# The state scan of a Mamba layer: all scan inputs made by TensorE from turned dt*u instead of half of them by VectorE

## The chip, the cores and the metric

One core of a Trainium2 chip runs one launch of a two-layer network. The metric is device time in microseconds (us) of that launch, the median of three runs. In the profile PE is TensorE (PEld its weight loads), DVE VectorE, ACT ScalarE, POOL GpSimd, SP the engine that issues the DMAs.

## The reference

The network is: normalisation, attention, normalisation, a mixture of experts; normalisation, a Mamba layer, normalisation, a second mixture of experts, on an input of 4 sequences x 1024 positions x 128 channels. The change touches the Mamba layer alone. Of it, this matters (256 inner channels, 16 states, rank 8):

```python
u = silu(causal_conv(xc))                          # (B, L, 256)
dt_low, Bm, Cm = split(u @ x_proj_w.T, [8, 24])    # 8, 16 and 16 columns
dt = softplus(dt_low @ dt_proj_w.T + dt_proj_b)    # (B, L, 256)
A = -exp(A_log)                                    # (256, 16)
for t in range(L):
    h = exp(dt[t][..., None] * A) * h + (dt[t] * u[t])[..., None] * Bm[t][:, None, :]
    y[t] = einsum('bdn,bn->bd', h, Cm[t])
y = (y + u * D) * silu(z)
```

## The kernel before, in words

Activations lie with channels on the 128 partitions and the 4096 tokens along the free axis; the 256 inner channels are two halves (`half` 0 and 1). Everything here is fp32 unless said otherwise. An fp32 product appears in the trace as two matmul records (two passes).

**`mamba_in`** (from line 1493) works in 8 chunks of 512 tokens. Its first part makes `u` and `silu(z)`. Its second part, called the dt stage here, makes B, C and dt. For a chunk TensorE projects `u` onto 40 low rows (`low_rank`, L1719), ScalarE stores the 32 rows of B and C (L1617), and again as bf16 (L1618); DVE and GpSimd split the rest of B and C into two further bf16 parts (L1667, L1570, L1678, L1680), so that `m.bc` holds three bf16 parts of each row. DVE copies the 8 rows of dt (`split`, L1663), TensorE projects them to 256 channels (`project_dt`, L1726) and turns the 16 rows of B into columns (L1730), ScalarE and DVE make the softplus (L1625, L1628, L1630; `join`, L1674), GpSimd adds it up (L1574). SP writes the rows of B and C to DRAM. Two banks hold the low rows in turn, and each engine is one chunk ahead with its early step (`ahead`).

**`mamba_scan`** (from line 1736) runs 4 sequences x 16 states = 64 states, two halves each, with 1024 positions along the free axis. For one state:

- ScalarE makes the decay exp(A dt) of each half (`decays`, L1903) and eight diagonal matrices with B on the diagonal (`diagonals`, L1883), one for each 128 positions.
- The input dt*u*B of half 0: TensorE spreads the row of B over all partitions with a selector matrix from the three bf16 parts (`spread`, L1800, two matmuls), and DVE multiplies it by dt*u in PSUM (`scan_input`, L1932).
- The input of half 1: TensorE multiplies the turned dt*u (128 positions on the partitions) by the diagonals (`make_x`, L1829, eight products 128x128).
- DVE runs one scan instruction for each half (L1942), from the decay in SBUF and the input in PSUM.
- GpSimd multiplies the states by the row of C (`weigh`, L1979); TensorE sums over states in PSUM through the identity (`add`, L1839, two products of 512 columns a half), and once a sequence adds u*D for each half (`skip`, L1846). After the 16th state DVE multiplies by silu(z) (`gate`, L1947).

The order on each engine is written out by hand. TensorE's for a pair of states is: `add` half 0, `spread`, `add` half 1, `make_x`, and the same again. SP loads the rows of C, broadcast to 128 partitions, into a ring of `C_RING` = 3. The decay has a buffer for each of two states and each half, the states `h` have the same in the memory of `xnT`; the input is in banks 0 to 3, the sums in banks 4 to 7. dt*u of the first sequence is made at the front of the block by DVE (L1927) and half 1 of it turned there (L1807); that of the next sequence is made by GpSimd (L1982) and turned tile by tile between the products (L1812, stored by ScalarE, L1897). The two semaphore waits that matter here:

```python
def spread(p, odd):   # TensorE, banks of half 0
    pe.wait_ge(scanned, ...)      # scan of half 0 of the state before
def make_x(p, odd):   # TensorE, banks of half 1
    pe.wait_ge(scanned, ...)      # scan of half 1 of the state before
```

## Time and profile before

| | us |
|---|---|
| median of 3 runs | 1429.58 (1429.04 to 1433.34) |
| the profiled execution | 1432.1 |
| its span, first to last instruction | 1430.3 |
| TensorE busy | 1268.5 (89%) |
| VectorE busy | 1111.4 (78%) |
| ScalarE busy | 830.7 (58%) |
| GpSimd busy | 590.2 (41%) |
| scan instructions (L1942), 128 | 287.0 |
| sums (L1839), 512 records | 241.5 |
| `make_x` (L1829), 1024 records | 127.7 |

Busy time says how full an engine is over the whole span, not what sets the pace of a stage; matmul records overlap, so the distance between the starts of two blocks tells what a block costs. The granted clock of TensorE has two levels, 1.2 and 2.4 GHz; 1.00 in the views is the upper one.

### The profile page before, as it was taken

How to read it: one execution, taken by the hardware profiler on the slowest of the kernel's cores; microseconds unless marked ns; L12 is line 12 of the kernel's file. 1: busy time of each engine (PE TensorE's matmuls, PEld its weight loads, DVE VectorE, ACT ScalarE, POOL GpSimd, SP SyncE). 2: the span in 40 equal slices, each digit the busy share in tenths (PEclk: the TensorE clock that was granted, in tenths of full speed). 3: DMA queues.
4: the chain of work that ended last, by engine and by line, in shares of the span. 5: the costliest groups of instructions: out<-in, count | busy, mean ns of one | idle time of the engine just before them, and what ended most of it. 6: DMA issues, size and time to landing. Idle time of an engine off the chain costs nothing. (4 is left out here: it accounts for less than half of the span.)

```text
span 1430.3 us, 23953 instructions
## 1 busy us (share of the span) xinstructions
PE 1268.5 (89%) x8534; PEld 662.8 (46%) x8534; DVE 1111.4 (78%) x1328; ACT 830.7 (58%) x1596; POOL 590.2 (41%) x442
## 2 busy tenths in 40 slices
PE   4937899999899889899978779999999999966998
PEld 2412333333334445354444235655656655555565
DVE  4769899999898547756555888989999999954554
ACT  2524899899798632132224788777778778502221
POOL 2320000010102166556744067788798788720000
PEclk9966999999999989999997878999999999985999
DMA  4331111311211173234420003222222222110221
GB/s 108 113 109 35 54 54 52 109 60 50 76 44 42 41 175 105 88 108 117 115 60 15 4 13 102 89 89 87 87 78 89 89 89 89 59 29 11 67 60 42
DMA packets 70751, 103.76 MB, mean 73 GB/s; under 512 B 12734, under 2 KB 42246, under 8 KB 70646
## 3 DMA queue, kind: packets, MB, share of 16 engines
q1 hardware_dynamic: 69350, 101.05, 23.4%
q10 hardware_dynamic: 1296, 1.33, 0.4%
q8 instruction: 64, 1.05, 0.3%
q14 instruction: 41, 0.34, 0.1%
HBM read 88.32 MB, written 13.63 MB: 71 GB/s over the span
## 5 line engine op out<-in xcount | busy, mean ns | idle before, releaser
L638 DVE TENSOR_REDUCE att_found<-PS 128x2 f32<-128x1024 f32 (+2 forms) x288 | 333.2, 1219 | 18.9 <-PE PS L747 17.1
L714 ACT ACTIVATE att_prob<-PS 128x512 f32<-128x512 f32 x576 | 313.5, 596 | 46.2 <-PE PS L769 34.4
L1979 POOL TENSOR_TENSOR ms_ch<-xnT,ms_c_rows 128x1024 f32<-128x1024 f32 x128 | 300.3, 2366 | 81.9 <-PE PS L1839 68.5
L1942 DVE TENSOR_TENSOR_SCAN xnT<-ms_decay,PS 128x1024 f32<-128x1024 f32 x128 | 287.0, 2276 | 17.6 <-PE PS L1829 8.7
L1839 PE MATMUL PS<-ms_ch,ident_sb 128*128 128x512 f32 x512 | 241.5, 594 | 1.2 <-POOL ms_ch L1979 1.2
L788 PE MATMUL PS<-att_prob,att_v 128*32 128x256 f32 (+1 forms) x2560 | 184.9, 376 | 2.8 <-ACT fr_out L703 2.6
L1903 ACT ACTIVATE ms_decay<-m_dt,m_a 128x1024 f32<-128x1024 f32 x128 | 145.8, 1144 | 54.8 <-DVE xnT L1942 53.3
L1883 ACT ACTIVATE ms_b_diag<-ident_sb,m_bt 128x128 f32<-128x128 f32 x512 | 155.7, 387 | 0.0
L747 PE MATMUL PS<-kr,qr 55*128 55x128 bf16 (+4 forms) x1152 | 121.4, 292 | 30.9 <-PEq L260 15.7
L1829 PEld LDWEIGHTS PS<-ms_b_diag,ms_dtu_turns 128*128 128x128 f32 x1024 | 122.6, 194 | 32.0 <-issue 29.7
L1829 PE MATMUL PS<-ms_b_diag,ms_dtu_turns 128*128 128x128 f32 x1024 | 127.7, 279 | 6.6 <-issue 5.4
L769 PE MATMUL PS<-qr,kr 55*128 55x128 bf16 (+4 forms) x1152 | 115.5, 279 | 15.2 <-ACT att_prob L714 8.3
L1839 PEld LDWEIGHTS PS<-ms_ch,ident_sb 128*128 128x128 f32 x512 | 91.7, 190 | 75.1 <-issue 61.7
L1262 ACT ACTIVATE f_h<-PS,e_w_b 128x512 f32<-128x512 f32 x64 | 44.0, 687 | 138.2 <-PE PS L1413 135.0
L747 PEld LDWEIGHTS PS<-kr,qr 48*128 48x128 bf16 (+1 forms) x1152 | 39.7, 97 | 138.2 <-issue 88.8
L1243 POOL TENSOR_TENSOR f_yT<-f_yT,f_prod 128x512 f32<-128x512 f32 x56 | 71.0, 1268 | 70.8 <-DVE f_prod L1355 69.4
L1345 DVE SCALAR_TENSOR_TENSOR f_x3s<-PS,e_w_b,f_mask_row 128x512 f32<-128x512 f32 x64 | 48.0, 750 | 61.5 <-PE PS L1417 60.8
L1231 POOL TENSOR_TENSOR f_xm<-xnT,f_gate_row 128x512 f32<-128x512 f32 x64 | 81.2, 1270 | 13.3 <-DMA f_gate_row<-gate_rows_dram 9.8
L788 PEld LDWEIGHTS PS<-att_prob,att_v 128*32 128x32 f32 x2560 | 55.2, 109 | 63.1 <-issue 53.9
L1932 DVE TENSOR_TENSOR PS<-ms_dtu,PS 128x1024 f32<-128x1024 f32 x64 | 77.4, 1210 | 4.5 <-PE PS L1800 2.4
L1422 PE MATMUL PS<-f_h,e_w_w 128*128 128x512 f32 x128 | 66.3, 599 | 8.5 <-DVE f_prod L1355 8.4
L1413 PE MATMUL PS<-f_xm,e_w_w 128*128 128x512 f32 x128 | 67.8, 612 | 4.1 <-POOL f_xm L1231 4.1
(232 smaller groups left out, 1634.6 us busy)
## 6 DMA issues: line engine op xcount, KB each, us to landing
ms_c_rows<-bc_rows_dram SPq DMA_DIRECT2D x64, 512.0 KB, 3.6
f_gate_row<-gate_rows_dram SPq DMA_DIRECT2D x64, 256.0 KB, 3.4
f_mask_row<-mask_rows_dram SPq DMA_DIRECT2D x64, 128.0 KB, 3.1
qk_parts_dram<-qkv_parts SPq DMA_DIRECT2D x48, 128.0 KB, 1.9
heads_dram<-fr_out SPq DMA_DIRECT2D x16, 256.0 KB, 2.6
f_mask_row<-mask_rows_dram SPq DMA_DIRECT2D x64, 64.0 KB, 3.2
qr<-qk_parts_dram SPq DMA_DIRECT2D x32, 96.0 KB
qr<-qk_parts_dram SPq DMA_DIRECT2D x96, 32.0 KB
```

Of the source, the lines that this page charges most:

```text
L638: dve.tensor_reduce(found[:, :, pair, first:first + (n - 1) * step + 1:step], PS[:, bank:bank + 2, :].rearrange("p r (w n) -> p r w n", w= ...
L714: act.activation(prob[:, step % PROB_RING * GH + h, :], PS[:, SCORE_BANK + unit % SCORE_RING, :], ACT.Exp, scale=float(D) ** -0.5).then_in ...
L747: last = pe.matmul(PS[:, MAX_BANK + 2 * (m % 2) + r, at:at + n], rows(qr, count, i, pair, r, q_block * P, P), rows(kr, count, i, pair, r, ...
L769: last[r] = pe.matmul(PS[:, SCORE_BANK + (unit + r) % SCORE_RING, col:col + w], rows(kr, count, i, pair, r, j * P, P), rows(qr, count, i, ...
L788: last = pe.matmul(PS[VW * h:VW * (h + 1), VALUE_BANK, q - half * CH:q - half * CH + w], v1[:, i % 2, half, h, j, :], prob[:, step % PROB_ ...
L1231: pool.tensor_tensor(xm[:, e % XM_RING, :], xnT[:, c * CH:(c + 1) * CH], gate_row[:, e % ROW_RING, :], ALU.mult).then_inc(xm_ready, 1)
L1829: last = pe.matmul(PS[:, X_BANK + 2 + k // TPC, k % TPC * P:(k % TPC + 1) * P], dtu_turns[:, b % 2, k, :], b_diag[:, odd, k, :], start=Tru ...
L1839: last = pe.matmul(PS[:, Y_BANK + 2 * half + q, :], g.ident[:, :], ch[:, half, q * CH:(q + 1) * CH], start=j == 0 and not odd, stop=j == J ...
L1883: last = act.activation(b_diag[:, odd, i, :], g.ident[:, :], ACT.Identity, scale=m.bt[:, at:at + 1])
L1903: act.activation(decay[:, odd, half, :], m.dt[:, half, sequence(p // JB)], ACT.Exp, scale=m.a[:, half, n:n + 1]).then_inc(decay_ready, 1)
L1942: dve.tensor_tensor_scan(h[:, odd, half, :], decay[:, odd, half, :], inputs(half), 0.0, ALU.mult, ALU.add).then_inc(scanned, 1)
L1979: pool.tensor_tensor(ch[:, half, :], h[:, odd, half, :], c_rows[:, s % C_RING, :], ALU.mult).then_inc(ch_ready, 1)
```

## The change

**dt stage.** The bf16 parts of B and C and the steps that made them go, and so does the selector matrix. Instead DVE multiplies dt by u for both halves of a chunk (`times_u`), one chunk late; TensorE turns both halves, eight transposes (`turn_dtu`), two chunks late; ScalarE stores the turns of half 0 and DVE those of half 1 (`store_turns`) in `m.dtu_turns`, which holds all 4096 tokens. The low rows have one bank instead of two. SP writes only the rows of C. The loops are written out.

**Scan.** `make_x` is called for both halves; `spread`, `scan_input`, the turning inside the scan and GpSimd's dt*u go. TensorE's order for a state is `make_x(s+1,0)`, `add(s-1,1)`, `make_x(s+1,1)`, `add(s,0)`, and `skip` follows the `add` of states 8 and 9. The decay and the states share one ring of three for each half, and the scan writes its result over its decay; `decays` waits for the weighing of three states before. The diagonals of a state are made in two groups of four, one behind each exponential. `gate` of a half follows the first scan of that half of the next sequence. `C_RING` is 4.

The core of `mamba_in` (lines that carry no step of the text are left out):

```diff
-C_RING = 3
+C_RING = 4
-    m.sel_b = m.tensor("sel_b", [6 * NS, NS, P], g.w["sel_b"], BF16)
...
-    m.bc = sb("bc", [6 * NS, N], BF16)
+    m.dtu_turns = sb("dtu_turns", [P, NT, DI, P])
...
+            def store_turns(c):
+                act.wait_ge(dtu_turned, DI * c + 1)
+                act.activation(m.dtu_turns[:, c * TPC:(c + 1) * TPC, 0, :], PS[:, DTU_BANKS[0], :].rearrange("p (i c) -> p i c", c=P),
+                               ACT.Copy).then_inc(dtu_stored[0], 1)
+
+            store_low(0)
+            for c in range(NCH):
+                if c + 1 < NCH:
+                    store_low(c + 1)
+                softplus(c)
+                if c >= 2:
+                    store_turns(c - 2)
...
+            def times_u(c):
+                dve.wait_ge(dt_ready, c + 1)
+                if c >= 2:
+                    dve.wait_ge(dtu_turned, DI * (c - 1))
+                dve.tensor_tensor(dtu[:, c % 2, :, :], m.dt[:, :, tokens(c)], m.u[:, :, tokens(c)], ALU.mult).then_inc(dtu_ready, 1)
+
+            def store_turns(c):
+                dve.wait_ge(dtu_turned, DI * c + 2)
+                dve.tensor_copy(m.dtu_turns[:, c * TPC:(c + 1) * TPC, 1, :], PS[:, DTU_BANKS[1], :].rearrange("p (i c) -> p i c", c=P)).then_inc(dtu_stored[1], 1)
+
+            split(0)
+            for c in range(NCH):
+                if c + 1 < NCH:
+                    split(c + 1)
+                join(c)
+                if c >= 1:
+                    times_u(c - 1)
+                if c >= 2:
+                    store_turns(c - 2)
+            times_u(NCH - 1)
...
-            def low_rank(b, k, c):
-                pe.wait_ge(rest_ready, c + 1)
+            def low_rank(c):
+                if c >= 1:
+                    pe.wait_ge(whole_ready, c)
+                    pe.wait_ge(low_ready, c)
                 for half in range(DI):
-                    last = pe.matmul(PS[0:2 * NS + R, LOW_BANK + k, :], x_proj[:, half, :], m.u[:, half, tokens(c)], start=half == 0, stop=half == DI - 1)
+                    last = pe.matmul(PS[0:2 * NS + R, LOW_BANK, :], x_proj[:, half, :], m.u[:, half, tokens(c)], start=half == 0, stop=half == DI - 1)
                 last.then_inc(low_done, 1)
 
-            def project_dt(b, k, c):
+            def project_dt(c):
+                k = c % 2
                 pe.wait_ge(low_ready, c + 1)
-                pe.wait_ge(top_ready, c + 1)
+                if c >= 2:
+                    pe.wait_ge(soft_steps, 3 * (c - 2) + 1)
+                    pe.wait_ge(top_ready, c - 1)
                 for half in range(DI):
                     last = pe.matmul(PS[:, DT_BANK + 2 * k + half, :], dt_proj[2 * NS:, half, :], low[2 * NS:, k, :], start=True, stop=True)
                 last.then_inc(dt_done, 1)
+
+            def turn_b(c):
                 pe.wait_ge(whole_ready, c + 1)
                 for i in range(TPC):
-                    last = pe.matmul(PS[:, TURN_BANK, bass.ds(c * (TPC * NS) + i * NS, NS)], bc_whole[0:NS, k, i * P:(i + 1) * P], g.ident[0:NS, 0:NS],
+                    last = pe.matmul(PS[:, B_BANK, (c * TPC + i) * NS:(c * TPC + i + 1) * NS], bc_whole[0:NS, c % 2, i * P:(i + 1) * P], g.ident[0:NS, 0:NS],
                                      start=True, stop=True)
                 last.then_inc(b_turned, 1)
-            ahead(pe, low_rank, project_dt)
+
+            def turn_dtu(c):
+                pe.wait_ge(dtu_ready, c + 1)
+                for half in range(DI):
+                    if c >= 1:
+                        pe.wait_ge(dtu_stored[half], c)
+                    for i in range(TPC):
+                        last = pe.transpose(PS[:, DTU_BANKS[half], i * P:(i + 1) * P], dtu[:, c % 2, half, i * P:(i + 1) * P], g.ident[:, :])
+                    last.then_inc(dtu_turned, 1)
+
+            low_rank(0)
+            for c in range(NCH):
+                if c + 1 < NCH:
+                    low_rank(c + 1)
+                project_dt(c)
+                turn_b(c)
+                if c >= 2:
+                    turn_dtu(c - 2)
+            for c in range(NCH - 2, NCH):
+                turn_dtu(c)
```

`mamba_scan`, with what is added and its frame (all of the old steps named above are removed):

```diff
 def mamba_scan(nc, g, m):
@@ -1740,226 +1777,125 @@
...
+        two_states, one_state = g.xnT[:, :].rearrange("p (k d t) -> p k d t", k=2, d=DI), sb("one_state", [P, DI, T])
...
+        diag, b_diag = sb("diag", [P, DI, P]), sb("b_diag", [P, 2, TB, P])
+        b_diag_ready, decay_ready, x_made, scanned, ch_ready, summed, gated, diag_ready = map(sem, (
+            "b_diag_ready", "decay_ready", "x_made", "scanned", "ch_ready", "summed", "gated", "diag_ready"))
         c_in = g.ring_in
...
+        STATES = B * NS
+        H_RING = 3
+        def decay_then_h(s, half):
+            r = s % H_RING
+            return two_states[:, r, half, :] if r < 2 else one_state[:, half, :]
         def sequence(b):
...
         def inputs(half):
...
         def sums(half):
...
+        def through(s, half):
+            return DI * s + half + 1
         @block.sync
         def _(sp):
...
+            for s in range(STATES):
...
+                    sp.wait_ge(ch_ready, through(s - C_RING, 1))
...
         @block.tensor
         def _(pe):
...
+            def make_x(s, half):
+                pe.wait_ge(b_diag_ready, through(s, 1))
+                if s > 0:
+                    pe.wait_ge(scanned, through(s - 1, half))
+                for k in range(TB):
+                    last = pe.matmul(PS[:, X_BANK + 2 * half + k // TPC, k % TPC * P:(k % TPC + 1) * P], m.dtu_turns[:, s // NS * TB + k, half, :],
+                                     b_diag[:, s % 2, k, :], start=True, stop=True)
+                last.then_inc(x_made, 1)
+            def add(s, half):
+                b, n = divmod(s, NS)
+                if n == 0 and b > 0:
+                    pe.wait_ge(gated, through(b - 1, half))
+                pe.wait_ge(ch_ready, through(s, half))
                 for q in range(CPB):
...
+                    last = pe.matmul(PS[:, Y_BANK + 2 * half + q, :], g.ident[:, :], ch[:, half, q * CH:(q + 1) * CH], start=n == 0, stop=n == NS - 1)
                 last.then_inc(summed, 1)
...
+                if n == NS // 2 + half:
+                    for q in range(CPB):
+                        pe.matmul(PS[:, Y_BANK + 2 * half + q, :], diag[:, half, :], m.u[:, half, b * T + q * CH:b * T + (q + 1) * CH], start=False, stop=False)
             pe.wait_ge(diag_ready, DI)
...
+            make_x(0, 1)
+            for s in range(STATES):
+                if s + 1 < STATES:
+                    make_x(s + 1, 0)
+                if s >= 1:
+                    add(s - 1, 1)
+                if s + 1 < STATES:
+                    make_x(s + 1, 1)
+                add(s, 0)
+            add(STATES - 1, 1)
         @block.scalar
         def _(act):
             act.preload_act_table(ACT.Exp)
...
+            def diagonals(s, part):
+                b, n = divmod(s, NS)
+                if s >= 2:
+                    act.wait_ge(x_made, through(s - 2, 1))
+                for i in range(part * TPC, (part + 1) * TPC):
...
+                    last = act.activation(b_diag[:, s % 2, i, :], g.ident[:, :], ACT.Identity, scale=m.bt[:, at:at + 1])
                 last.then_inc(b_diag_ready, 1)
...
+            def decays(s, half):
+                b, n = divmod(s, NS)
+                if s >= H_RING:
+                    act.wait_ge(ch_ready, through(s - H_RING, half))
+                act.activation(decay_then_h(s, half), m.dt[:, half, sequence(b)], ACT.Exp, scale=m.a[:, half, n:n + 1]).then_inc(decay_ready, 1)
+            for part in range(CPB):
+                diagonals(0, part)
+            for s in range(STATES):
+                for half in range(DI):
+                    decays(s, half)
+                    if s + 1 < STATES:
+                        diagonals(s + 1, half)
         @block.vector
         def _(dve):
...
+            def scan(s, half):
+                dve.wait_ge(decay_ready, through(s, half))
+                dve.wait_ge(x_made, through(s, half))
+                dve.tensor_tensor_scan(decay_then_h(s, half), decay_then_h(s, half), inputs(half), 0.0, ALU.mult, ALU.add).then_inc(scanned, 1)
             def gate(b, half):
...
+                dve.wait_ge(summed, through(NS * b + NS - 1, half))
                 dve.tensor_tensor(u, sums(half), m.sz[:, half, sequence(b)], ALU.mult).then_inc(gated, 1)
...
+            for s in range(STATES):
+                b, n = divmod(s, NS)
+                for half in range(DI):
+                    scan(s, half)
+                    if n == 0 and b > 0:
+                        gate(b - 1, half)
             for half in range(DI):
...
             dve.wait_ge(gated, DI * B)
@@ -1969,30 +1905,13 @@
             for half in range(DI):
                 pool.tensor_tensor(diag[:, half, :], g.ident[:, :], m.d[:, half:half + 1].to_broadcast([P, P]), ALU.mult).then_inc(diag_ready, 1)
...
+            for s in range(STATES):
+                pool.wait_ge(c_in[s % C_RING], C_BASE + 16 * (s // C_RING + 1))
+                for half in range(DI):
+                    pool.wait_ge(scanned, through(s, half))
+                    if s >= 1:
+                        pool.wait_ge(summed, through(s - 1, half))
+                    pool.tensor_tensor(ch[:, half, :], decay_then_h(s, half), c_rows[:, s % C_RING, :], ALU.mult).then_inc(ch_ready, 1)
```

## Rows read from the trace of the kernel before

**Rows 1.** Busy time by stage: us, busy (and count) by engine, PEclk, DMA share, GB/s

```profile
813.00:856.90 43.90, 36.48 (x128) 14.73 (x128) 31.16 (x49) 36.28 (x52) 22.11 (x16) 0.77 0.05 12
...
840.50:856.90 16.40, 9.63 (x27) 4.43 (x25) 11.09 (x18) 12.84 (x18) 10.58 (x7) 0.50 0.03 8
856.90:867.80 10.90, 7.38 (x28) 5.54 (x28) 7.53 (x5) 10.88 (x23) 4.09 (x3) 0.50 0.50 146
867.80:1257.80 390.00, 380.01 (x1700) 226.79 (x1700) 364.32 (x198) 287.92 (x645) 311.61 (x133) 1.00 0.24 83
```

**Rows 2.** Timeline of TensorE, one state: start us, us, engine, line, operation, count

```profile
1044.97 1.95 PE L1829 MATMUL PS<-ms_b_diag,ms_dtu_turns 128*128 128x128 f32 x16
1046.76 1.88 PE L1839 MATMUL PS<-ms_ch,ident_sb 128*128 128x512 f32 x4
1048.47 0.60 PE L1800 MATMUL PS<-m_bc,m_w_sel_b 96*128 96x512 bf16 x2
1048.91 1.88 PE L1839 MATMUL PS<-ms_ch,ident_sb 128*128 128x512 f32 x4
1050.63 1.61 PE L1829 MATMUL PS<-ms_b_diag,ms_dtu_turns 128*128 128x128 f32 x13
```

**Rows 3.** Timeline of DVE, the same stretch

```profile
1045.00 4.46 DVE L1942 TENSOR_TENSOR_SCAN xnT<-ms_decay,PS 128x1024 f32<-128x1024 f32 x2
1049.39 1.21 DVE L1932 TENSOR_TENSOR PS<-ms_dtu,PS 128x1024 f32<-128x1024 f32 x1
1050.72 2.29 DVE L1942 TENSOR_TENSOR_SCAN xnT<-ms_decay,PS 128x1024 f32<-128x1024 f32 x1
```

**Rows 4.** Waits of the scan: who waited for whom: us in total, times, longest

```profile
PEld PS L1800 <- DVE xnT L1942: 20.4, 35, 1.7
```

**Rows 5.** Timelines of ScalarE and GpSimd, the same stretch

```profile
1044.84 2.43 ACT L1883 ACTIVATE ms_b_diag<-ident_sb,m_bt 128x128 f32<-128x128 f32 x8
1047.33 1.15 ACT L1903 ACTIVATE ms_decay<-m_dt,m_a 128x1024 f32<-128x1024 f32 x1
...
1048.81 4.69 POOL L1979 TENSOR_TENSOR ms_ch<-xnT,ms_c_rows 128x1024 f32<-128x1024 f32 x2 [0.97 <-PE PS L1839]
```

**Rows 6.** Timeline of the front of the scan block

```profile
856.91 1.28 ACT L1874 ACT_TABLE_LOAD   x1 [2.78 <-PEq L1498]
...
856.95 2.81 DVE L1927 TENSOR_TENSOR ms_dtu<-m_dt,m_u 128x1024 f32<-128x1024 f32 x2 [2.79 <-PEq L1498]
858.21 2.45 ACT L1883 ACTIVATE ms_b_diag<-ident_sb,m_bt 128x128 f32<-128x128 f32 x8
...
862.70 3.78 PE L1829 MATMUL PS<-ms_b_diag,ms_dtu_turns 128*128 128x128 f32 x16 [1.23 <-ACT ms_dtu_turns L1889]
```

**Rows 7.** Timeline of the end of the scan block

```profile
1246.01 1.95 PE L1829 MATMUL PS<-ms_b_diag,ms_dtu_turns 128*128 128x128 f32 x16
...
1256.57 1.23 DVE L1947 TENSOR_TENSOR m_u<-PS,m_sz 128x1024 f32<-128x1024 f32 x1 [1.08 <-PE PS L1839]
```

**Rows 8.** Timeline of the dt stage

```profile
820.32 1.91 PE L1719 MATMUL PS<-m_u,m_w_x_proj 128*40 x4
...
821.73 1.41 DVE L1674 TENSOR_SCALAR mi_xc<-PS,m_w_dt_b 128x512 f32<-128x512 f32 x2 [1.16 <-ACT mi_conv L1625]
...
823.78 0.57 ACT L1617 ACTIVATE mi_bc_whole<-PS 32x512 f32<-32x512 f32 x1
...
824.07 1.91 PE L1719 MATMUL PS<-m_u,m_w_x_proj 128*40 x4
...
828.04 0.57 ACT L1617 ACTIVATE mi_bc_whole<-PS 32x512 f32<-32x512 f32 x1
```

**Rows 9.** The instructions of line 1574: shortest/median/longest ns, first and last start

```profile
L1574 POOL TENSOR_TENSOR m_dt<-mi_xc,mi_conv x8: 2002/2234/2454, 824.1 to 853.9; 128x1024 f32 x8
```

**Rows 10.** DMA issues before the scan: out<-in, queue, count, size

```profile
m_w_sel_b<-sel_b SPq DMA_DIRECT2D x1, 384.0 KB
```

**Rows 11.** Busy time after the scan, columns as in rows 1

```profile
1290.00:1430.00 140.00, 121.77 (x553) 81.61 (x553) 68.78 (x120) 30.23 (x49) 0.20 (x1) 0.89 0.19 46
```

More of the change, by code:

```diff
@@ L1561, in _ @@
                                ALU.add).then_inc(pool_seen, 1)
[L1563 to L1574 removed]
+            for c in range(NCH):
+                pool.wait_ge(top_ready, c + 1)
+                pool.wait_ge(soft_steps, 3 * (c + 1))
+                pool.tensor_tensor(m.dt[:, :, tokens(c)], top[:, c % 2, :, :], soft[:, c % 2, :, :], ALU.add).then_inc(dt_ready, 1)
         @block.scalar
@@ L1784, in c_row @@
                 sp.dma_start(c_rows[:, s % C_RING, :], g.bc_rows[NS + s % NS:NS + s % NS + 1, sequence(s // NS)].to_broadcast([P, T])).then_inc(c_in[s % C_RING], 16)
-            for p in range(PAIRS_ALL):
-                c_row(p, 0)
-                c_row(p, 1)
         @block.tensor
         def _(pe):
-            def spread(p, odd):
-                n, b = 2 * p % NS + odd, p // JB
-                if odd:
-                    pe.wait_ge(scanned, scans(p, 0, 0))
-                elif p > 0:
-                    pe.wait_ge(scanned, scans(p - 1, 1, 0))
-                for q in range(CPB):
-                    last = pe.matmul(PS[:, X_BANK + q, :], m.sel_b[:, n, :], m.bc[:, b * T + q * CH:b * T + (q + 1) * CH], start=True, stop=True)
-                last.then_inc(b_spread, 1)
@@ L1833, in add @@
-            def add(p, odd, half):
-                b, j = divmod(p, JB)
-                if j == 0 and not odd and b > 0:
-                    pe.wait_ge(gated, DI * (b - 1) + half + 1)
-                pe.wait_ge(ch_ready, scans(p, odd, half))
-                for q in range(CPB):
-                    last = pe.matmul(PS[:, Y_BANK + 2 * half + q, :], g.ident[:, :], ch[:, half, q * CH:(q + 1) * CH],
-                                     start=j == 0 and not odd, stop=j == JB - 1 and bool(odd))
+            def make_x(s, half):
[6 more added lines that the diff above has]
+                last.then_inc(x_made, 1)
@@ L1899, in decays @@
-            def decays(p, odd, half):
-                if p > 0:
-                    act.wait_ge(scanned, scans(p - 1, odd, half))
-                n = 2 * p % NS + odd
-                act.activation(decay[:, odd, half, :], m.dt[:, half, sequence(p // JB)], ACT.Exp, scale=m.a[:, half, n:n + 1]).then_inc(decay_ready, 1)
-            diagonals(0, 0)
-            decays(0, 0, 0)
-            first_turns()
-            decays(0, 0, 1)
-            diagonals(0, 1)
-            decays(0, 1, 0)
-            decays(0, 1, 1)
@@ L1924, in _ @@
+            for part in range(CPB):
[5 more added lines that the diff above has]
+                        diagonals(s + 1, half)
         @block.vector
         def _(dve):
-            def times_u(half, ready):
-                dve.tensor_tensor(dtu[:, half, :], m.dt[:, half, sequence(0)], m.u[:, half, sequence(0)], ALU.mult).then_inc(ready, 1)
-            def scan_input(p, odd):
-                dve.wait_ge(dtu_ready, p // JB + 1)
-                dve.wait_ge(b_spread, states(p, odd))
-                dve.tensor_tensor(inputs(0), dtu[:, 0, :], inputs(0), ALU.mult).then_inc(input_ready, 1)
@@ L1934, in scan @@
-            def scan(p, odd, half):
-                if p > 0:
-                    dve.wait_ge(ch_ready, scans(p - 1, odd, half))
-                dve.wait_ge(decay_ready, scans(p, odd, half))
-                if half:
-                    dve.wait_ge(x_made, states(p, odd))
-                else:
-                    dve.wait_ge(input_ready, states(p, odd))
-                dve.tensor_tensor_scan(h[:, odd, half, :], decay[:, odd, half, :], inputs(half), 0.0, ALU.mult, ALU.add).then_inc(scanned, 1)
+            def scan(s, half):
+                dve.wait_ge(decay_ready, through(s, half))
+                dve.wait_ge(x_made, through(s, half))
+                dve.tensor_tensor_scan(decay_then_h(s, half), decay_then_h(s, half), inputs(half), 0.0, ALU.mult, ALU.add).then_inc(scanned, 1)
```

233 lines of the change are left out of this document (39 added, 194 removed).

## The prediction

> **What bounds the kernel now.** I read the stages first, then one steady state, then the stage edges. The change touches two stages. The dt stage of `mamba_in` takes 43.9 us and runs partly at full, partly at half clock; the scan block takes 400.9 us, from 856.9 to the end of the last gate (1256.57 + 1.23 = 1257.8), and from 867.8 on it has the full clock throughout, with TensorE busy 380.0 of 390.0 us and DVE 364.3 [rows 1]. So both engines are nearly full, and the question is which one sets the pace of a state.
>
> One steady state answers it [rows 2]. TensorE has four blocks: `make_x` (8 products 128x128, 16 passes) from 1044.97 to 1046.76 = 1.79 us, `add` of one half to 1048.47 = 1.71, `spread` to 1048.91 = 0.44, `add` of the other half to 1050.63 = 1.72. Each block starts as the one before it runs out, and together they are 5.66 us. DVE in the same stretch repeats after 5.72 us: two scans (4.46) and the multiplication of half 0 (1.21) [rows 3]. DVE is 0.06 us the longer. Its scan of half 0 sometimes ends too late for `spread`, but mostly that only stops a weight load from going ahead [rows 4]. What the reader is to see: TensorE has no room. 64 states by 5.72 are 366 us, `skip` is 8 blocks of the form of an `add`, 8 x 1.72 = 13.8, and the rest of the 400.9 are the front, the tail and three sequence changes.
>
> **The change part by part, scan.**
> *Removed:* the `spread` block, 0.44 us a state on TensorE; the DVE multiplication, 1.21 a state; the turns inside the scan (24 transposes, and 8 at its front) with their ScalarE copies; GpSimd's dt*u. DVE falls from 5.72 to 4.46 a state. This gains time only if nothing else is then longer.
> *Added:* `make_x` for half 0, as many products of the same form as half 1 has now, so 1.79 us a state more on TensorE. New sum of TensorE: 2 x 1.79 + 1.71 + 1.72 = 7.01 us a state. Nothing hides it, because the blocks already touch each other. ScalarE does what it did, two exponentials and eight diagonals, 2 x 1.15 + 2.43 = 4.73 [rows 5]; GpSimd two weighings, 4.69 [rows 5]. Both stay under 7.01, so TensorE alone sets the pace, 1.29 us a state above now.
> *Moved, and the waits:* each block waits for something that has been ready for long. I laid the new order out: `make_x(s+1,0)` at 0, `add(s-1,1)` at 1.79, `make_x(s+1,1)` at 3.50, `add(s,0)` at 5.29. The scan of (s+1,0) runs from about 1.9 to 4.2 and is wanted at 7.01; that of (s+1,1) from 5.4 to 7.7 and is wanted at 10.5; GpSimd starts (s+1,0) after `add(s,0)`, at 7.2, and has it by 9.6, wanted at 12.3. The ring of three moves the exponentials' wait from `scanned` of two states ago to `ch_ready` of three states ago, the diagonals' wait to `x_made` of two states ago: both lie over 5 us back. SP fetches a row of C a ring of four ahead instead of three, so earlier than now. The scan now writes over its own decay; no row shows that form. Below nothing it cannot go, since DVE is not the pace, and TensorE's slack covers it up to 7.01 - 4.46 = 2.5 us a state: taken as 0.
> *Sequence changes:* `gate` (1.2 us) stands behind the first scan and waits for the sums, and the second scan stands behind it. By the same layout, `make_x(s+1,1)` is some 0.2 us late: 3 x 0.2 = 0.6.
> *Front:* table load 1.28 and diagonals 2.45 first, since `make_x(0,0)` needs them. At half clock a `make_x` is 3.78 [rows 6]; two of them end at 11.3, the second half's scan at 13.7, the next `make_x` pair and `add` at 17.3.
> *Tail:* last `make_x` to last gate is about 10 us now (1246.01 + 1.79 to 1257.8 [rows 7]), the same chain of weighings, sums and gates remains: 10.0.
> Sum: 17.3 + 62 x 7.01 (434.6) - 1.7 (the last `add` lies in the tail) + 13.8 + 0.6 + 10.0 = 474.6, against 400.9: **+73.7 us**.
>
> **The change part by part, dt stage.** Now a chunk takes 4.27 us there (823.78 to 828.04 between two stores of the low rows [rows 8]), set by ScalarE; TensorE needs 3.75 (820.32 to 824.07 [rows 8]). Gone are one ScalarE copy, three DVE steps, one GpSimd cast; a ScalarE copy of turned dt*u takes the copy's place, so ScalarE keeps 4.27. DVE: 0.68 for the split as now, 1.41 for the join [rows 8], 1.41 for dt*u (2.81 for two [rows 6]) and about 0.68 for a store of turns = 4.2. TensorE gets eight transposes, each 0.11 apart (as the 16 passes of a `make_x`, 1.79 / 16 [rows 2]), 0.9 in all: 4.65, with exposed loads 4.7. So TensorE becomes the bound: 7 x 0.43 = 3.0. With one bank for the low rows `low_rank(1)` waits for store and split: 0.9. And after the last dt (2.45 on GpSimd, as now) come times_u 1.41, transposes 0.9, a store 0.68: 3.0. That is +6.9 at full clock; what leaves DVE and GpSimd also shortens the last chain, which may give 2.5 back (4.4). If the last two chunks and turns run at half clock, as 840.5 to 856.9 does now [rows 1], TensorE needs about 9 a chunk: 9 more, 16. I take **+8**, nearer the full-clock sum since the traffic is denser. The 384 KB of the selector are not loaded any more [rows 10]; the first product that reads them starts at 858.7, so nothing waited for them: 0. SP writes the C rows alone, 16 of 32: 0. Unrolled loops: no row prices them, taken as 0.
>
> One rule speaks against this step. `times_u` on DVE has two inputs in SBUF and will run while GpSimd adds up dt. Row first: GpSimd's eight adds of dt took 2.00 to 2.45 us while DVE was at two-input steps of its own, so 0.45 us is the most that anything beside them cost [rows 9], and GpSimd's result is wanted only a chunk later: I charge 0. The Trainium skill (SBUF — State Buffer, "SBUF: two separate sides") says that a DVE operation with two SBUF inputs and a GpSimd operation that reads SBUF lock each other out for a whole instruction. By that rule, taken at its worst with the 2.23 us of an add before each `times_u`, DVE would need 6.4 us a chunk instead of TensorE's 4.7, 12 more over seven chunks, and the total would be +93.7, still inside the range.
>
> Total: 73.7 + 8 = +81.7. The sum is against the profiled execution (1432.1 us, span 1430.3); the median of the runs is 1429.58, 0.2% below, and the stages are taken as the same there. 1429.58 + 81.7 = **1511 us**.
>
> **The rivals.**
> *Forecast, TensorE as bound at 7.01: chance 0.90.* For: touching blocks, 380 of 390 us busy.
> *Clock lost in the scan, slower still: 0.06.* More than half of TensorE's time would be 128-column passes. If the clock fell once in each sequence for as long as it did before the scan (840.5 to 867.8, 27.3 us), each would cost 13.7: +55, 1566 us. Against: full clock for 390 us, through 63 bursts of the same passes [rows 1]. The Trainium skill (TensorE: Matmul & The Clock Gate, "HAM oscillation — how this bites in real kernels") tells of a kernel whose short matmul bursts, with waits between them, lost the full clock again and again; by that rule this time would follow if waits opened between the blocks, and the trace shows none.
> *Faster: TensorE's records are not its pace, 0.03.* Matmul ends are modelled, and TensorE could be following DVE. Then the state would go to the longest other engine, ScalarE's 4.73: 17.3 + 62 x 4.73 + 22.7 = 333, -68 in the scan, +8 before it: 1370 us. It decides where a `make_x` block takes under (4.73 - 3.43) / 2 = 0.65 us. Against: starts, not ends, give 1.79, in a state where TensorE waits for nobody [rows 2].
> *No change: 0.01.* If the second set of products were not issued after all, a state would take TensorE's 5.66 without `spread` and DVE's 4.46 or ScalarE's 4.73; only if something not seen here held it at today's pace, 5.72, would the dt stage's +8 and the scan's shorter changes leave it near 1433. The diff shows the products issued.
>
> **How the numbers follow.** Low end: front at full clock (two `make_x` 2 us shorter each, -3.6) and dt stage +4.4 give 1504; the stages after the scan run at a mean clock of 0.89 [rows 11] and start 80 us later, so their half-clock stretches may fall otherwise by some 3 us either way: 1500. High end: one exposed block head a state (the records of `make_x` last 1.95 where the next block starts after 1.79, so 0.16 x 62 = 9.9 [rows 2]) and dt stage +16: 1529, and the same 3: 1532. About 0.85 lies inside. Faster by over 0.3% (about what a measurement of this kernel can tell from no change) 0.03, within 0.01, slower 0.96.
>
> **What would show it.** Right: scans of half 0 7.0 us apart; DVE idle about 2.5 us a state on the products of `make_x`; TensorE busy over 95% of a scan of about 475 us at clock 1.0; DVE about 80 us less busy; GpSimd waiting for `add`. Wrong: spacing of 5.7 or less, gaps in TensorE's blocks, or a scan that waits for its decay.

## The result and the profile after

The changed kernel takes 1509.08 us (median of 4 runs, 1505.54 to 1516.21) against 1429.9 of the kernel before on the same chip: ratio 1.0555, 95% interval 1.0512 to 1.0599, slower. The profiled execution took 1505.54 us, its span is 1503.7.

Busy time by stage after the change, columns as in [rows 1]. The stretches are the dt stage, the scan block up to the full clock, and the rest of the scan block.

```profile
808.03:857.86 49.83, 43.33 (x192) 21.48 (x192) 30.96 (x41) 36.85 (x51) 18.91 (x8) 0.84 0.02 6
857.86:867.69 9.83, 5.89 (x32) 5.73 (x32) 2.07 (x1) 9.18 (x20) 0.76 (x2) 0.58 0.72 215
867.69:1331.23 463.54, 460.31 (x2560) 327.85 (x2560) 299.30 (x136) 281.66 (x621) 302.01 (x128) 1.00 0.20 69
```

TensorE is busy for 460.3 of 463.5 us at full clock; DVE fell from 364.3 busy of 390 us to 299.3 of 463.5. The span splits like this:

| us | before | after | difference |
|---|---|---|---|
| up to the dt stage | 813.1 | 808.0 | -5.1 |
| dt stage | 43.8 | 49.9 | +6.1 |
| scan block to its last gate | 400.9 | 473.4 | +72.5 |
| after it | 172.5 | 172.5 | 0.0 |
| span | 1430.3 | 1503.7 | +73.4 |

The first line has the same code in both kernels but for the load of the selector. Between the runs of the experiments below, the start of the dt stage lies anywhere from 806.2 to 813.3 us; it is scatter, and the profiled execution is the fastest of the four. Against the median (1509.08 - 1429.9 = 79.2) the account is +6.1 and +72.5.

One state, TensorE's timeline after:

```profile
1050.96 1.95 PE L1825 MATMUL PS<-ms_b_diag,m_dtu_turns 128*128 128x128 f32 x16
1052.75 1.88 PE L1835 MATMUL PS<-ms_ch,ident_sb 128*128 128x512 f32 x4
1054.47 1.72 PE L1825 MATMUL PS<-ms_b_diag,m_dtu_turns 128*128 128x128 f32 x14
```

The blocks still touch, as in [rows 2]: `make_x` 1.79 from start to start, `add` 1.72, then the second `make_x`. There are two of each a state. DVE's timeline of one state shows the same pace: two scans of half 0 start at 1012.76 and 1019.77, with one of half 1 between them, and each scan is preceded by an idle wait for TensorE:

```profile
1012.76 2.29 DVE L1886 TENSOR_TENSOR_SCAN xnT<-xnT,PS 128x1024 f32<-128x1024 f32 x1 [1.22 <-PE PS L1825]
1016.27 2.29 DVE L1886 TENSOR_TENSOR_SCAN xnT<-xnT,PS 128x1024 f32<-128x1024 f32 x1 [1.22 <-PE PS L1825]
1019.77 2.29 DVE L1886 TENSOR_TENSOR_SCAN xnT<-xnT,PS 128x1024 f32<-128x1024 f32 x1 [1.22 <-PE PS L1825]
```

The scans of half 0 are 7.01 us apart in nearly all states of the program; the two states a sequence with a D*u block take 8.72. The waits of the scan block (who waited for whom: us in total, times, longest) say the same from the other side:

```profile
ACT ms_b_diag L1864 <- PE PS L1825: 163.6, 60, 4.2
POOL ms_ch L1914 <- PE PS L1835: 157.9, 125, 2.9
DVE xnT L1886 <- PE PS L1825: 98.6, 74, 2.9
...
DVE ms_one_state L1886 <- PE PS L1825: 51.4, 38, 2.9
```

Before, DVE's scans waited 8.7 us in all for `make_x`; now they wait 98.6 + 51.4 = 150 us, and the other two engines wait as long for TensorE. TensorE itself waits 1.4 us in this stretch, 1.2 for GpSimd and 0.2 for a scan.

### The profile page after: what moved, and what is told of

Same layout as the page of the kernel before. It is cut to its first block and busy times, and to the rows that moved or that the text cites. A ratio compares the mean times of both kernels' runs of the same rounds, so it can differ in the third digit from the quotient of the medians.

```text
span 1503.7 us, 25474 instructions
## 1 busy us (share of the span) xinstructions
PE 1352.5 (90%) x9462; PEld 769.8 (51%) x9462; DVE 1041.6 (69%) x1254; ACT 823.3 (55%) x1570; POOL 574.1 (38%) x428
## 3 DMA queue, kind: packets, MB, share of 16 engines
q8 instruction: 72, 1.18, 0.3%
## 5 line engine op out<-in xcount | busy, mean ns | idle before, releaser
L1825 PEld LDWEIGHTS PS<-ms_b_diag,m_dtu_turns 128*128 128x128 f32 x2048 | 250.0, 193 | 67.3 <-issue 65.6
L1886 DVE TENSOR_TENSOR_SCAN xnT<-xnT,PS 128x1024 f32<-128x1024 f32 x86 | 196.2, 2285 | 107.2 <-PE PS L1825 106.9
L1825 PE MATMUL PS<-ms_b_diag,m_dtu_turns 128*128 128x128 f32 x2048 | 251.7, 276 | 6.0 <-ACT ms_b_diag L1864 5.2
L1864 ACT ACTIVATE ms_b_diag<-ident_sb,m_bt 128x128 f32<-128x128 f32 x512 | 162.5, 388 | 164.3 <-PE PS L1825 164.2
L1914 POOL TENSOR_TENSOR ms_ch<-xnT,ms_c_rows 128x1024 f32<-128x1024 f32 x86 | 203.0, 2361 | 113.7 <-PE PS L1835 104.3
L747 PE MATMUL PS<-kr,qr 55*128 55x128 bf16 (+4 forms) x1152 | 121.6, 292 | 31.1 <-PEq L260 15.9
L1886 DVE TENSOR_TENSOR_SCAN ms_one_state<-ms_one_state,PS 128x1024 f32<-128x1024 f32 x42 | 95.9, 2286 | 51.5 <-PE PS L1825 51.4
L1835 PEld LDWEIGHTS PS<-ms_ch,ident_sb 128*128 128x128 f32 x512 | 87.6, 191 | 64.5 <-issue 61.7
L1914 POOL TENSOR_TENSOR ms_ch<-ms_one_state,ms_c_rows 128x1024 f32<-128x1024 f32 x42 | 99.0, 2358 | 53.6 <-PE PS L1835 53.6
L1871 ACT ACTIVATE xnT<-m_dt,m_a 128x1024 f32<-128x1024 f32 x86 | 97.4, 1134 | 0.0
```

The costliest lines, as they stand in the source:

```text
L747: last = pe.matmul(PS[:, MAX_BANK + 2 * (m % 2) + r, at:at + n], rows(qr, count, i, pair, r, q_block * P, P), rows(kr, count, i, pair, r, ...
L1825: last = pe.matmul(PS[:, X_BANK + 2 * half + k // TPC, k % TPC * P:(k % TPC + 1) * P], m.dtu_turns[:, s // NS * TB + k, half, :], b_diag[: ...
L1835: last = pe.matmul(PS[:, Y_BANK + 2 * half + q, :], g.ident[:, :], ch[:, half, q * CH:(q + 1) * CH], start=n == 0, stop=n == NS - 1)
L1864: last = act.activation(b_diag[:, s % 2, i, :], g.ident[:, :], ACT.Identity, scale=m.bt[:, at:at + 1])
L1871: act.activation(decay_then_h(s, half), m.dt[:, half, sequence(b)], ACT.Exp, scale=m.a[:, half, n:n + 1]).then_inc(decay_ready, 1)
L1886: dve.tensor_tensor_scan(decay_then_h(s, half), decay_then_h(s, half), inputs(half), 0.0, ALU.mult, ALU.add).then_inc(scanned, 1)
```

## The experiments

Stage times below are read from each kernel's trace; the scan block runs from the load of its activation table to the end of its last DVE step. Spacing is the time from one scan of half 0 to the next; a sequence change is the step from one sequence's 16th state to the next one's first. Ratios are to the kernel before on the same chip. **The theory**: a state takes as long as the engine with the longest sum of work in it. **Rivals**: TensorE's records are not its pace and DVE leads; TensorE alone matters; the waits of the new order and its rings are the pace.

**b_no_mult: the kernel before without DVE's multiplication.** Left out: half 0's input is the spread row of B and lacks dt*u.

```diff
-                dve.tensor_tensor(inputs(0), dtu[:, 0, :], inputs(0), ALU.mult).then_inc(input_ready, 1)
+                dve.sem_inc(input_ready, 1)
```

> Kernel before, with DVE's multiplication of half 0 by dt*u left out (the scan of half 0 reads the spread row of B alone). DVE's work falls from 5.72 to 4.46 us a state, TensorE's stays 5.66. Theory (a state takes the longest engine's sum of work): scans of half 0 are 5.66 apart, the total falls by 0 to 6 us, to about 1427. Rival (DVE sets the pace and TensorE only follows it): 4.73 a state, ScalarE's work, the total falls by some 60 us to about 1370.

Measured: 1427.68 us, ratio 0.9972 (0.9955 to 0.9989). The scan block is 396.6 us, 4.3 less, and the states are 5.66 apart, 5.77 where a tile is turned (one transpose, 0.11). TensorE's timeline of two such states:

```profile
988.40 0.27 PE L1812 MATMUL PS<-ident_sb,ms_dtu 128*128 128x128 f32 x1
988.51 1.95 PE L1829 MATMUL PS<-ms_b_diag,ms_dtu_turns 128*128 128x128 f32 x16
990.30 1.88 PE L1839 MATMUL PS<-ms_ch,ident_sb 128*128 128x512 f32 x4
992.02 0.60 PE L1800 MATMUL PS<-m_bc,m_w_sel_b 96*128 96x512 bf16 x2
992.46 1.88 PE L1839 MATMUL PS<-ms_ch,ident_sb 128*128 128x512 f32 x4
994.17 0.27 PE L1812 MATMUL PS<-ident_sb,ms_dtu 128*128 128x128 f32 x1
```

From 988.40 to 994.17 every block begins as the one before runs out. 77 us of DVE work, taken away altogether, are worth 4. With TensorE's work as it was, that is all the change could have won from DVE.

**b_no_spread: the kernel before without the spread products.** Left out: from the second state on, the row of B is not spread, and half 0's input is a difference of old values.

```diff
+                if p > 0 or odd:
+                    pe.sem_inc(b_spread, 1)
+                    return
                 for q in range(CPB):
                     last = pe.matmul(PS[:, X_BANK + q, :], m.sel_b[:, n, :], m.bc[:, b * T + q * CH:b * T + (q + 1) * CH], start=True, stop=True)
...
-                dve.tensor_tensor(inputs(0), dtu[:, 0, :], inputs(0), ALU.mult).then_inc(input_ready, 1)
+                dve.tensor_tensor(inputs(0), dtu[:, 0, :], inputs(0), ALU.mult if p == 0 and not odd else ALU.subtract).then_inc(input_ready, 1)
```

> Kernel before, with the two spread products left out in every state but the first, and DVE's multiplication of half 0 turned into a subtraction of the same form on what lies in the banks. TensorE's work falls from 5.66 to 5.22 us a state, DVE's stays 5.72. Theory: 5.72 apart as before; only the states with the D*u blocks get cheaper, total down by 3 to 8 us. A rival in which TensorE alone sets the pace: 5.22 a state, total down by 28 us or more.

Measured: 1421.36 us, ratio 0.9937 (0.9915 to 0.9958). Scan block 392.6, 8.3 less. The plain states stay 5.72 apart, DVE's sum; what is gained lies in the states with D*u (5.72, 5.94, 6.55 instead of 6.50, 5.82, 7.38) and at the sequence changes. At the front two states are 0.6 longer than before (6.28 and 6.32). TensorE alone is not the pace either.

**b_neither: both left out.** As in the two kernels above.

> Kernel before, with both left out: the multiplication of half 0 and the spread products in every state but the first. Theory: both engines bound the state, so only together do they give: TensorE 5.22, DVE 4.46, so 5.22 a state, 0.50 x 64 = 32 us less, about 1398. Rival (DVE as the pace): ScalarE's 4.73, about 1366. Rival (waits between engines as the pace): about as either alone, some 1425.

Measured: 1409.03 us, ratio 0.9842 (0.9805 to 0.9879). Scan block 376.4: 24.5 less, where the two alone gave 4.3 + 8.3 = 12.6. Plain states are 5.22 apart, as expected, so the theory holds for them and both rivals fall. The forecast of 32 us less was still too large, and the spacing shows why: 5.33 in seven of the eight states with a transpose, 7.05 in the eighth, which also has a D*u block, and 8.57 at a sequence change. Work that had stood beside the longer engine is on the path once the states are short.

**b_twice: the kernel before with each product of `make_x` issued twice.**

```diff
-                    last = pe.matmul(PS[:, X_BANK + 2 + k // TPC, k % TPC * P:(k % TPC + 1) * P], dtu_turns[:, b % 2, k, :], b_diag[:, odd, k, :],
-                                     start=True, stop=True)
+                    for again in range(2):
+                        last = pe.matmul(PS[:, X_BANK + 2 + k // TPC, k % TPC * P:(k % TPC + 1) * P], dtu_turns[:, b % 2, k, :], b_diag[:, odd, k, :],
+                                         start=True, stop=True)
```

> Kernel before, with every product of make_x issued twice into the same place (the second overwrites the first, the result is the same). TensorE 5.66 + 1.79 = 7.45 us a state, everything else as before. Theory: 7.45 apart, 64 x 1.73 = 111 more, less some 6 that the other waits at sequence changes lose: about 1535. This is the added work of the change without its ring, order, turns and waits. Rival (TensorE's records are not its pace): the extra passes fit below DVE's 5.72 at least in part, clearly under 1500.

Measured: 1541.94 us, ratio 1.0781 (1.0746 to 1.0816); scan block 511.0, 110.1 more. Spacing 7.44 (7.55 with a transpose). TensorE's timeline:

```profile
1007.31 1.88 PE L1840 MATMUL PS<-ms_ch,ident_sb 128*128 128x512 f32 x4
1009.03 3.73 PE L1830 MATMUL PS<-ms_b_diag,ms_dtu_turns 128*128 128x128 f32 x32
1012.60 1.88 PE L1840 MATMUL PS<-ms_ch,ident_sb 128*128 128x512 f32 x4
```

Thirty-two passes take 3.57 us, twice 1.79. The added work of the change has its full price in the old order too. It came to 110 us where 105 was expected: transposes and D*u blocks that had stood partly beside DVE's longer sum are now on the path (7.55 and 9.21 instead of 5.72 and 6.50).

**a_half: the changed kernel with four of half 0's eight products.** Left out: the other four tiles of half 0's input keep the values of the first state.

```diff
-                for k in range(TB):
+                for k in range(TB if half or s == 0 else TPC):
```

> Kernel after, with only four of the eight products of half 0 made in every state but the first (the other four tiles keep old values). TensorE 7.01 - 0.90 = 6.12 us a state. Theory: 6.12 apart, 63 x 0.895 = 56 us less than the changed kernel, about 1453. Rival (the waits of the new order are the pace, not TensorE's work): no or little change from 1509.

Measured: 1456.66 us, ratio 1.0173 (1.013 to 1.0215), 52 us below the changed kernel. Spacing 6.11, scan block 421.3, 52.1 less than after. TensorE's timeline:

```profile
1001.49 1.05 PE L1825 MATMUL PS<-ms_b_diag,m_dtu_turns 128*128 128x128 f32 x8
1002.38 1.88 PE L1835 MATMUL PS<-ms_ch,ident_sb 128*128 128x512 f32 x4
1004.10 1.95 PE L1825 MATMUL PS<-ms_b_diag,m_dtu_turns 128*128 128x128 f32 x16
```

A plain state follows TensorE's work, pass by pass. A sequence change with the two states behind it shrank by less (9.60 + 4.37 + 5.60 instead of 9.80 + 4.55 + 7.01, 1.8 and not 2.7), and so did the front, hence 52 and not 56.

**a_dve_work: the changed kernel with the DVE multiplication put back.** Changed: half 0's input is multiplied by dt once more.

```diff
                 dve.wait_ge(x_made, through(s, half))
+                if half == 0:
+                    dve.tensor_tensor(inputs(0), m.dt[:, 0, sequence(s // NS)], inputs(0), ALU.mult).then_inc(multiplied, 1)
+                    dve.wait_ge(multiplied, s + 1)
```

> Kernel after, with a DVE multiplication put back before each scan of half 0, of the same form as the one removed (dt times the input, in PSUM; half 0 is thereby multiplied by dt once more). DVE 4.46 + 1.21 = 5.7 us a state, under TensorE's 7.01. Theory: no change in a steady state (7.01), 0 to 6 us more in all at sequence changes, 1509 to 1515. Rival (DVE's freed time is worth something): up to 77 us more.

Measured: 1511.38 us, ratio 1.0562 (1.0517 to 1.0607); spacing 7.01, scan block 478.6 (5.2 more, at front and sequence changes). Putting 79 us of DVE work back costs 5 us at the edges and nothing in a steady state, so what the change took off DVE is worth 5 us at most under the new order.

**a_rings_old: the changed kernel with the old depths of rings.**

```diff
-        H_RING = 3
+        H_RING = 2
-C_RING = 4
+C_RING = 3
```

> Kernel after, with a ring of two for decay and state instead of three, and a ring of three for the rows of C instead of four. Theory: with TensorE as the pace neither is needed: a decay may begin when the weighing of two states ago is done, about 9 us before the scan that wants it. 7.01 apart, total the same within the runs (1505 to 1516). Rival (the ring carries the new order): exponentials late, scans waiting for their decay, more than 7.2 a state.

Measured: 1509.99 us, ratio 1.0545 (1.0501 to 1.0589); spacing 7.01, scan block 473.7 against 473.4. The third buffer and the fourth row of C are worth 0.3 us together in these profiles, next to nothing. In this profile the dt stage took 58.5 us instead of 49.9, at a mean clock of 0.70 instead of 0.84. The busy times of that stage in a_rings_old, columns as in [rows 1]:

```profile
806.20:864.70 58.50, 51.80 (x192) 24.25 (x192) 30.96 (x41) 37.24 (x52) 18.88 (x8) 0.70 0.02 5
```

In a_half it took 56.6 at 0.74. The other profiles of the changed kernel and its variants have 49.9. The same instructions take 7 to 9 us longer when most of their first 24 us fall at 1.2 GHz: the granted clock of those 24 us was 0.52 in a_rings_old, 0.64 in a_half and 0.93 in the changed kernel. The last 11 to 12 us ran at 0.50 in all three.

**a_skip_dve: the changed kernel with D*u on DVE.**

```diff
-                if n == NS // 2 + half:
-                    for q in range(CPB):
-                        pe.matmul(PS[:, Y_BANK + 2 * half + q, :], diag[:, half, :], m.u[:, half, b * T + q * CH:b * T + (q + 1) * CH], start=False, stop=False)
...
-                dve.tensor_tensor(u, sums(half), m.sz[:, half, sequence(b)], ALU.mult).then_inc(gated, 1)
+                dve.scalar_tensor_tensor(u, u, m.d[:, half:half + 1], sums(half), ALU.mult, ALU.add).then_inc(skipped, 1)
+                dve.wait_ge(skipped, DI * b + half + 1)
+                dve.tensor_tensor(u, u, m.sz[:, half, sequence(b)], ALU.mult).then_inc(gated, 1)
```

> Kernel after, with D*u taken off TensorE: the eight blocks go, and DVE adds u*D to the sums in one more instruction at each gate (the result is the same). Theory: TensorE has 8 x 1.72 = 13.8 us less; DVE has 8 x 1.2 = 10 us more, of which those at the three sequence changes and the last two stand in the way for perhaps 5: total 8 us less, about 1501, with all states 7.01 apart but those at sequence changes. Rival (total work counts, whatever the engine): 4 us less.

Measured: 1512.69 us, ratio 1.0567 (1.0518 to 1.0615), a miss: 8 us less were expected, and the scan block is 475.0, 1.6 more than after. All states are 7.01 apart, so TensorE did get 13.8 us less, but the spacing at a sequence change rose from 9.80 to 14.38. DVE's timeline at a change:

```profile
984.59 1.28 DVE L1889 SCALAR_TENSOR_TENSOR m_u<-m_u,m_w_d,PS 128x1024 f32<-128x1024 f32 x1 [2.87 <-PE PS L1836]
985.90 2.27 DVE L1891 TENSOR_TENSOR m_u<-m_u,m_sz 128x1024 f32<-128x1024 f32 x1
988.10 2.27 DVE L1884 TENSOR_TENSOR_SCAN xnT<-xnT,PS 128x1024 f32<-128x1024 f32 x1
990.30 1.25 DVE L1889 SCALAR_TENSOR_TENSOR m_u<-m_u,m_w_d,PS 128x1024 f32<-128x1024 f32 x1
991.58 2.32 DVE L1891 TENSOR_TENSOR m_u<-m_u,m_sz 128x1024 f32<-128x1024 f32 x1
```

GpSimd's timeline in the same stretch of a_skip_dve:

```profile
984.72 2.37 POOL L1914 TENSOR_TENSOR ms_ch<-xnT,ms_c_rows 128x1024 f32<-128x1024 f32 x1 [1.17 <-PE PS L1836]
990.45 2.36 POOL L1914 TENSOR_TENSOR ms_ch<-xnT,ms_c_rows 128x1024 f32<-128x1024 f32 x1 [3.37 <-DVE xnT L1884]
```

The multiplication by silu(z), both inputs in SBUF, ends at 988.17 and 993.90: each time 1.08 to 1.09 us after GpSimd's weighing has ended (987.09 and 992.81). Its shortest execution, after the last weighing, is 1.224 us. All six multiplications at the three changes do this (2.27 to 2.32). The 4.58 us more at a change are the two multiplications whole, 2.27 + 2.32: 2.45 of it is the work itself, standing ahead of a scan, and 2.14 the wait beside GpSimd.

The longer waits did something else too. TensorE's timeline at the first and at the last change, and the busy times of a stretch behind the first, columns as in [rows 1]:

```profile
990.52 3.01 PE L1826 MATMUL PS<-ms_b_diag,m_dtu_turns 128*128 128x128 f32 x16 [2.47 <-DVE xnT L1884]
991.30:994.70 3.40, 3.40 (x14) 2.70 (x13) 3.37 (x3) 1.13 (x4) 1.51 (x1) 0.51 0.21 57
1224.57 2.02 PE L1826 MATMUL PS<-ms_b_diag,m_dtu_turns 128*128 128x128 f32 x16 [2.47 <-DVE xnT L1884]
```

TensorE waits 2.47 us for a scan at each of the three changes. At the first two the granted clock then falls to 1.2 GHz for 3.4 us, from 991.3 and from 1107.4 (the `make_x` of 990.52 takes 2.81 instead of 1.79); at the last it stays at 2.4. The spacing is 14.38 or 14.39 at all three, so this fall cost nothing: DVE was the path there.

**a_skip_pool: the same with the second product on GpSimd.** It goes in pieces of 512 columns, one in each of four states of the next sequence, behind both weighings; the last sequence's stays on DVE.

```diff
+                dve.scalar_tensor_tensor(u, u, m.d[:, half:half + 1], sums(half), ALU.mult, ALU.add).then_inc(gated, 1)
+                if b == B - 1:
+                    dve.wait_ge(gated, DI * b + half + 1)
+                    dve.tensor_tensor(u, u, m.sz[:, half, sequence(b)], ALU.mult).then_inc(finished, 1)
...
+                if b > 0 and 4 <= n < 8:
+                    at, q = divmod(n - 4, CPB)
+                    part = slice((b - 1) * T + q * CH, (b - 1) * T + (q + 1) * CH)
+                    pool.wait_ge(gated, DI * (b - 1) + at + 1)
+                    pool.tensor_tensor(m.u[:, at, part], m.u[:, at, part], m.sz[:, at, part], ALU.mult).then_inc(finished_pool, 1)
```

> Kernel after, with D*u off TensorE as in a_skip_dve, but the multiplication by silu(z) goes to GpSimd in pieces of 512 (as in b_gate) and DVE keeps one instruction a gate; for the last sequence DVE does both. The result is the same. In a_skip_dve the spacing at a sequence change rose from 9.80 to 14.38 us, because the DVE multiplication with both inputs in SBUF took 2.27 us beside GpSimd's weighing and 1.22 without it. Theory (that instruction waits until GpSimd's is over, and it stands ahead of a scan): without it at the changes the spacing is 9.8 to 9.9 again, the scan block 473.4 - 13.8 + 1.5 = 461 us instead of 475.0, total about 1497. Rival (the second instruction or the wait for the sums is what costs, wherever the product is made): 12 us or more at a change, total 1505 or above.

Measured: 1494.43 us, ratio 1.0438 (1.04 to 1.0477). Spacing at a change 9.86, scan block 461.4, forecast 461. The theory holds: the second DVE instruction at the changes was the cost. This run takes the whole instruction away, so it does not separate its work from its wait beside GpSimd; the timelines above do (2.45 and 2.14).

**b_gate: the kernel before with D*u off TensorE.** TensorE's `skip` is removed; the gate is as in a_skip_pool; `finish` is its multiplication of 512 columns of u by silu(z), which GpSimd does between two pairs of weighings:

```diff
                 weigh(p, 0, 1)
+                if b > 0 and 2 <= j < 6:
+                    finish(b - 1, (j - 2) // CPB, (j - 2) % CPB)
```

> Kernel before, with D*u taken off TensorE: the eight blocks go; the gate on DVE becomes u*D + sums in one instruction, and GpSimd, which has 1.0 us a state free, multiplies by silu(z) later in pieces of 512 (1.27 us, one in each of four pairs of states); for the last sequence DVE does it. The result is the same. Theory (the states with D*u blocks are TensorE-bound, all others are balanced): the four to five late states of a sequence (6.5, 5.8, 5.8, 7.4 apart instead of 5.72) go back to 5.72, 2.6 x 4 = 10 us less, up to 2 us back in the tail and what the pieces cost where GpSimd is late: 1421 to 1425, faster than both kernels. Rival (GpSimd's slack is not there when it is wanted): each piece delays a state by up to 1.2, 12 pieces, 14 us more, so 1430 or above.

Measured: 1419.95 us (1415.65 to 1421.51), ratio 0.9923 (0.9902 to 0.9944): 0.8% faster than the kernel before and the only variant whose result is unchanged that beats it; 1 us below what was expected (1421 to 1425). Scan block 389.4, 11.5 less. The spacing is 5.72 in all states but the first and those at a change (8.83), also where GpSimd has a piece. The timeline of such a state in b_gate:

```profile
1019.21 1.26 POOL L1982 TENSOR_TENSOR m_u<-m_u,m_sz 128x512 f32<-128x512 f32 x1
...
1020.41 1.88 PE L1840 MATMUL PS<-ms_ch,ident_sb 128*128 128x512 f32 x4
1020.43 4.67 POOL L1974 TENSOR_TENSOR ms_ch<-xnT,ms_c_rows 128x1024 f32<-128x1024 f32 x2
1021.54 1.21 DVE L1924 TENSOR_TENSOR PS<-ms_dtu,PS 128x1024 f32<-128x1024 f32 x1
```

GpSimd begins its next weighing at 1020.43, 5.89 us after the one at 1014.54, where its pace is 5.72; it is 0.17 late, and nothing behind it moves.

## Why the prediction was right, point by point

- **The new pace.** Forecast 7.01 us a state with TensorE as the bound; measured 7.01. It came from distances between block starts in one undisturbed state; b_twice and a_half confirm the price in both kernels. The sign "DVE about 80 us less busy" came out as 70: 371.9 before and 301.4 after in the scan block, mostly since the scans no longer run in pairs and take 2.29 each instead of 2.23.
- **DVE's saving is worth nothing.** Forecast from two sums within 0.06 us; b_no_mult (4 us for the whole step) and a_dve_work (7.01 unchanged, 5 us at the edges) confirm it. The pace before was not TensorE's or DVE's but both: alone they give 4.3 and 8.3 us, together 24.5.
- **The scan block.** Forecast 474.6, measured 473.4. Front: forecast 17.3, measured 15.9 (from 857.88 to the end of the first `add`, at 873.81, where the next block begins), since the full clock came back at 866.1, during the second `make_x`, where the forecast had both at half clock. Sequence changes: forecast 0.2 each, measured 9.80 + 4.55 - 14.02 = 0.33. Tail: 10.0 and 10.0 (1319.47 + 1.79 to 1331.25). The errors of 1.4 and 1.0 us in front and changes have opposite signs.
- **Scan in place and rings, taken as 0.** The scan that writes over its decay takes 2.29 us as before; the rings are worth 0.3 us (a_rings_old).
- **The dt stage.** Forecast +8 between 4.4 and 16; measured +6.1 in four profiles and +13 to +15 in two. All lie inside the range, but the long ones not for the reason given for its high end. That was the last two chunks at half clock, 9 us more; measured, the end of the stage ran at 1.2 GHz in the short stage and in the long ones alike, and what made the long ones long was 1.2 GHz at the start. That the range covers them is partly luck. Single terms were off: times_u took 1.22 us, not 1.41. A chunk is 4.77 us (824.11 to 828.88 between two groups of transposes), forecast 4.7.
- **The other rivals.** The clock stayed at 2.4 GHz for the whole scan of the changed kernel from 866.1 on. In two variants it did fall inside the scan block, each time for 3.4 us behind a wait of TensorE of about 2.5 us: in a_skip_dve at two of three sequence changes, and in b_neither once at the front, from 870.2. So the rival's way exists; its size, 13.7 us a sequence, occurred in no run, and the changed kernel has no such waits in its steady states. The faster rival is refuted by b_twice.
- **The port.** I charged 0 for `times_u` beside GpSimd. In the dt stage that was right for the path, but the reason was weak: the 0.45 us between GpSimd's adds were taken as all that such neighbours can cost, and a_skip_dve shows 1.05 to 1.09 us for a DVE instruction. The 0.45 were misread as well. GpSimd's adds alternate between two lengths 0.35 us apart, one for even and one for odd chunks, and the rest goes with the overlap. The timeline of the changed kernel's dt stage shows both lengths:

```profile
826.90 1.22 DVE L1681 TENSOR_TENSOR mi_dtu<-m_dt,m_u 128x1024 f32<-128x1024 f32 x1
827.76 2.21 POOL L1561 TENSOR_TENSOR m_dt<-mi_xc,mi_conv 128x1024 f32<-128x1024 f32 x1 [1.49 <-ACT mi_conv L1618]
...
831.72 1.22 DVE L1681 TENSOR_TENSOR mi_dtu<-m_dt,m_u 128x1024 f32<-128x1024 f32 x1
832.58 2.57 POOL L1561 TENSOR_TENSOR m_dt<-mi_xc,mi_conv 128x1024 f32<-128x1024 f32 x1 [2.60 <-ACT mi_conv L1618]
```

Here `times_u` runs 0.36 us into each add, and the adds take 2.22 and 2.57. In the kernel before, a DVE step with two SBUF inputs (L1680) runs 0.15 us into most of them, and they take 2.01 and 2.36; in the last two it runs 0.25 us into them, and they take 2.11 and 2.45. So in either series the add is longer by as much as the overlap is: GpSimd is held until the DVE step ends. `times_u` begins 0.86 to 0.89 us before the add each time, so it keeps its 1.22 us, and the worst case of the forecast, the add first, never arose. The add's result is wanted later, so the path did not feel it. Why the two series differ is not shown. One add does not fit: the first of the changed kernel has no such DVE step beside it and takes 2.00, where its series would give 1.86.

## What to carry to other kernels

Two engines that both come out at nearly the same sum per step bound it together: taking work from one is worth only the distance to the other (here 0.06 us of 1.21), and moving it onto the other costs its full price. Measure a block by the distance between starts in a state where the engine waits for nobody, add the blocks for the new order, and compare the engines before writing any code. Here the gain, 0.8% in b_gate, was in the work that disturbed only some states, and it had to go to the engine with idle time.

## What the runs showed of the hardware

- In a_skip_dve a DVE multiplication with both inputs in SBUF, issued 1.13 to 1.18 us into a GpSimd weighing, ended 1.08 to 1.09 us after it in all six cases and took 2.27 to 2.32 us instead of 1.22. The other way round, GpSimd's adds grow by the time that such a DVE step runs into them (2.01, 2.11 and 2.22 us at 0.15, 0.25 and 0.36). DVE steps with one input in PSUM were not lengthened beside a weighing: the scan 2.25 to 2.29 as without it, the gate of the changed kernel 1.22, the gate of a_skip_dve 1.25 to 1.28 against 1.27 alone. The Trainium skill (SBUF — State Buffer, "SBUF: two separate sides") says so: such a DVE operation and the GpSimd operation exclude each other for a whole instruction; by that rule, the traces agree in both directions.
- The same dt stage took 49.9 or 56.6 to 58.5 us by where its start fell among the stretches of the clock at 1.2 GHz. It could account for most of the 10.7 us between the fastest and slowest run of the changed kernel, but this is not shown: only profiled executions tell the clock by stage.
- After a wait of about 2.5 us in an otherwise full TensorE the granted clock fell to 1.2 GHz for 3.4 us in some cases (a_skip_dve at two changes, b_neither at the front) and not in another of the same length (a_skip_dve, 1222.1 to 1224.6).
